# Another order of setup work in a transformer block kernel: fills and later modulations behind the first score operands

## The reference

```python
mod = (silu(c) @ wmod).reshape(8, 6, 1, 256)
sa, ca, ga, sb, cb, gb = (mod[:, i] for i in range(6))
ga, gb = (where(g >= 0, 1, -1) * maximum(abs(g), 0.25) for g in (ga, gb))
h = layernorm(x) * (1 + ca) + sa
x = x + ga * attention(h)        # 16 heads of 16 channels, softmax over 512 keys
h = layernorm(x) * (1 + cb) + sb
x = x + gb * moe(h)              # 2 shared and 16 routed experts, gelu, top 4 of 16
```

## Time and profile before

| | |
|---|---|
| time, median of 3 runs (lowest, highest) | 909.97 us (909.76, 910.23) |
| the profiled execution | 910.85 us |
| its span from first to last instruction | 909.0 us |
| PE busy | 846.5 us, 93% |
| DVE busy | 645.1 us, 71% |
| ACT busy | 665.0 us, 73% |
| POOL busy | 396.6 us, 44% |
| chain that ended last | PE 65%, DVE 18%, ACT 9%, POOL 4% |

### The profile page before, as it was taken

How to read it: one execution, slowest core, us unless ns; L and a number is a source line. 1 busy time by engine, 2 the same in 40 slices (tenths; PEclk the granted TensorE clock), 3 DMA queues, 4 the chain that set the end, 5 groups by cost and what they waited for, 6 DMA issues and landing times.

```text
span 909.0 us, 19413 instructions
## 1 busy us (share of the span) xinstructions
PE 846.5 (93%) x7652; PEld 450.6 (50%) x7652; DVE 645.1 (71%) x1252; ACT 665.0 (73%) x1125; POOL 396.6 (44%) x331
## 2 busy tenths in 40 slices
PE   4878887999999999999999999999999999998998
PEld 4322133365445555565545555566555554555455
DVE  7856577677688878777788777876787778544332
ACT  3488777878788788878788787788886777854342
POOL 5373224234544453444635453444535253347353
PEclk9988889999999999999999999999999999999999
DMA  7043500531217102450217102450233300420140
GB/s 252 2 115 104 140 1 30 175 66 48 76 54 206 52 1 89 129 145 26 83 53 206 48 19 82 147 141 13 70 113 105 111 2 3 151 94 1 64 154 25
DMA packets 47290, 77.18 MB, mean 85 GB/s; under 512 B 6392, under 2 KB 41432, under 8 KB 43104
## 3 DMA queue, kind: packets, MB, share of 16 engines
q1 hardware_dynamic: 47200, 75.94, 27.3%
HBM read 63.47 MB, written 12.34 MB: 83 GB/s over the span
## 4 chain that ended last, share of the span: by engine, by line
PE 65%; DVE 18%; ACT 9%; issue 4%; POOL 4%; ACTq 0%; DVEq 0%; POOLq 0%
PE scalar_bank L945 18%; PE down_bank L1106 17%; DVE neg_max L902 7%; PE vector_bank L1025 6%; PE vector_bank L1008 6%; PE scalar_bank L1008 6%; PE vector_bank L945 5%; DVE rows L758 3%; ACT q_aug L692 3%; DVE gelu L889 2%; PE scalar_bank L1037 2%; POOL act_lo L650 2%; PE vector_bank L1043 2%; ACT gelu L741 2%; DVE o_raw L893 1%
## 5 line engine op out<-in xcount | busy, mean ns | idle before, releaser
L902 DVE TENSOR_REDUCE neg_max<-vector_bank 128x1 f16<-128x512 f32 x484 | 305.8, 684 | 51.3 <-PE vector_bank L1008 44.6
L706 ACT ACTIVATE probs<-scalar_bank 128x512 f32<-128x512 f32 x486 | 260.5, 603 | 48.8 <-PE scalar_bank L1008 44.5
L650 POOL TENSOR_TENSOR act_lo<-gelu,act_hi 128x512 f16<-128x512 f32 x144 | 180.7, 1275 | 136.4 <-ACT act_hi L683 123.1
L1106 PE MATMUL down_bank<-down_hi,act_hi 64*128 64x256 f16 x1120 | 179.1, 270 | 1.9 <-DVE rows L877 1.5
L1106 PE MATMUL down_bank<-down_hi,act_lo 64*128 64x256 f16 x1120 | 178.2, 269 | 0.0
L1106 PE MATMUL down_bank<-down_lo,act_hi 64*128 64x256 f16 x1120 | 178.2, 269 | 0.0
L889 DVE TENSOR_TENSOR gelu<-gelu,gates 128x512 f32<-128x512 f32 x128 | 116.7, 928 | 65.8 <-ACT gelu L741 65.2
L1008 PE MATMUL vector_bank<-k_aug,q_aug 64*128 64x512 f16 x484 | 133.6, 392 | 11.1 <-DVE neg_max L902 6.0
L1008 PE MATMUL scalar_bank<-q_aug,k_aug 64*128 64x512 f16 x486 | 134.2, 387 | 5.2 <-ACT f_ring L669 2.4
L741 ACT ACTIVATE gelu<-scalar_bank 128x512 f32<-128x512 f32 x144 | 84.7, 596 | 70.5 <-PE scalar_bank L945 39.4
L1025 PE MATMUL vector_bank<-probs,v_aug 128*32 128x512 f32 x992 | 118.5, 601 | 0.0
(11 more groups left out here) (193 smaller groups left out, 1259.6 us busy)
## 6 DMA issues: line engine op xcount, KB each, us to landing
gates<-gates_by_expert SPq DMA_DIRECT2D x32, 1024.0 KB, 4.9
q_aug<-q_parts SPq DMA_DIRECT2D x90, 64.0 KB, 3.4
k_aug<-k_parts SPq DMA_DIRECT2D x90, 64.0 KB, 4.1
x_pre<-in_x SPq DMA_DIRECT2D x8, 512.0 KB, 5.9
x_post<-in_x SPq DMA_DIRECT2D x8, 512.0 KB, 5.4
out<-x_post SPq DMA_DIRECT2D x16, 256.0 KB, 2.5
gates<-in_w_up SPq DMA_DIRECT2D x4, 576.0 KB, 10.6
gates<-in_w_down SPq DMA_DIRECT2D x4, 576.0 KB, 3.9
```

The costliest lines, as they stand in the source:

```text
L650: pool.tensor_tensor(act[1][:, c, :], gelu[:, n % NGELU, :], act[0][:, c, :], ALU.subtract).then_inc(s_elo, 1)
L706: scalar.activation(probs[:, n % U, :], src[:], ACT.Exp, scale=SCALE).then_inc(taken[kind], 1)
L902: dve.tensor_reduce(neg_max[:, (u // 2) % TT, at:at + 1], src[:], AX.X, ALU.max, negate=True).then_inc(done, 1)
L1106: ins = pe.matmul(o, act[a][at:at + 64, act_slot(b, c), tok:tok + P], wd[w][at:at + 64, c, :], start=n == 0 and k == 0, stop=c == NEX - 1 ...
```

## The change

Nothing is computed otherwise; instructions change their place or their engine.

- POOL's fills of `q_aug[1]` and `k_aug[1]` move from setup into a new item `fill`, placed at 3.0 of the first group, and POOL also fills `v_aug` there, with two instructions where DVE had eight.
- `late` leaves `HEAD` and is placed at 4.0 of the first group. The q and k bias matmuls leave it for PE's setup, between `modulations(0)` and `h1T`. The second half of the weights' low parts (`w4_lo(1)`) joins `late` on DVE.
- The fourfold identity is made by ACT instead of DVE. DVE finishes silu ahead of the selection columns.
- `bqk` is loaded third instead of sixth, on a semaphore of its own.

```diff
-HEAD = [("x_pre", 0, 1), ("h1T", 0, 0), ("h1T", 1, 0), ("late", 0, 0), ("first", 0, 0), ("first", 1, 0), ("first", 2, 0), ("first", 3, 0)]
+HEAD = [("x_pre", 0, 1), ("h1T", 0, 0), ("h1T", 1, 0), ("first", 0, 0), ("first", 1, 0), ("first", 2, 0), ("first", 3, 0)]
-EARLY = {("first", 4): 3.35, ("first", 5): 5.32, ("first", 6): 9.51, ("first", 7): 11.99, ("qk", 2): 11.62, ("qk_out",
+EARLY = {("late", 0): 4.0, ("fill", 0): 3.0, ("first", 4): 3.35, ("first", 5): 5.32, ("first", 6): 9.51, ("first", 7): 11.99, ("qk", 2): 11.62, ("qk_out",
...
+            sp.dma_start(bqk[:], bqk_in).then_inc(s_bqk, 16)
             mods = wmod.rearrange("(c p) n -> p c n", c=DC)
...
-            pool.memset(q_aug[1][:].bitcast(U32), 0).then_inc(s_aug1, 1)
-            pool.memset(k_aug[1][:].bitcast(U32), 0x3C003C00).then_inc(s_aug1, 1)
...
+                if kind == "fill":
+                    pool.memset(q_aug[1][:].bitcast(U32), 0).then_inc(s_aug1, 1)
+                    pool.memset(k_aug[1][:].bitcast(U32), 0x3C003C00).then_inc(s_aug1, 1)
+                    for m in v_aug:
+                        pool.memset(m[:], 1.0).then_inc(s_aug1, 1)
...
+            scalar.wait_ge(s_const, 6)
+            scalar.activation(four_times(ident_wide), ident[:].rearrange("p (h d) -> p h d", d=DH).unsqueeze(2).broadcast_to([P, 8, 4, DH]),
+                              ACT.Copy).then_inc(s_rep, 1)
...
                 if kind == "late":
+                    w4_lo(1)
                     dve.wait_ge(s_setup_mm, 2)
...
-                    for n in range(2):
-                        for kc in range(TT):
-                            dve.memset(v_aug[n][:, kc, :], 1.0).then_inc(s_aug1, 1)
...
             pe.wait_ge(s_const, 7)
+            pe.wait_ge(s_rep, 1)
+            pe.wait_ge(s_bqk, 16)
+            for pair in range(4):
+                ins = pe.matmul(DB[1][:, 2 * pair:2 * pair + 2], ident_wide[:, P * pair:P * (pair + 1)], bqk[:, 0:4:2], start=True, stop=True)
+            ins.then_inc(s_pickT, 1)
```

More of the change, by code:

```diff
@@ L427, in block_kernel @@
         s_w4, s_mod_in = [sem("wqk_loaded"), sem("wvo_loaded")], [sem("mod0_loaded"), sem("mod1_loaded")]
-        s_small, s_w4hi = sem("biases_loaded"), sem("w4_hi")
+        s_bqk, s_small, s_w4hi = sem("qk_biases_loaded"), sem("biases_loaded"), sem("w4_hi")
         s_w4s, s_silu, s_setup_mm, s_setup_v = sem("w4_split"), sem("silu_steps"), sem("mods_made"), sem("setup_vector")
@@ L497, in _ @@
                              wqkvo[2 * m:2 * m + 2].rearrange("w (c p) n -> p (w c) n", c=DC)).then_inc(s_w4[m], 16)
-            sp.dma_start(bqk[:], bqk_in).then_inc(s_small, 16)
             sp.dma_start(bv_all[:], bv.partition_broadcast(P)).then_inc(s_small, 16)
@@ L523, in _ @@
                         sp.wait_ge(s_aug0, 2)
-                        sp.wait_ge(s_aug1, 2 + 2 * TT)
+                        sp.wait_ge(s_aug1, 4)
                     wait(sp, s_qkst[t], 64, b, 32 * m)
@@ L607, in _ @@
                 z, x_post = z2[b % 2], x_post2[b % 2]
-                if kind == "wsplit":
+                if kind == "fill":
[3 more added lines that the diff above has]
+                        pool.memset(m[:], 1.0).then_inc(s_aug1, 1)
+                elif kind == "wsplit":
                     pool.wait_ge(s_whi, n + 1)
@@ L759, in ln_rows @@
                                       ALU.subtract, ALU.mult).then_inc(s_ln, 1)
+            dve.wait_ge(s_silu, 1)
+            dve.tensor_scalar(silu_t, silu_t, 1.0, None, ALU.add).then_inc(s_silu, 1)
+            dve.wait_ge(s_silu, 2)
+            dve.reciprocal(silu_t, silu_t).then_inc(s_silu, 1)
+            dve.wait_ge(s_silu, 3)
+            dve.tensor_tensor(silu, silu_t, ct_st, ALU.mult).then_inc(s_silu, 1)
             dve.wait_ge(s_const, 6)
-            dve.tensor_copy(four_times(ident_wide), ident[:].rearrange("p (h d) -> p h d", d=DH).unsqueeze(2).broadcast_to([P, 8, 4, DH])
-                            ).then_inc(s_rep, 1)
             dve.tensor_reduce(pick[:, 0:4, 0], ident[:].rearrange("p (x r d) -> p r x d", x=2, r=4), AX.XY, ALU.add).then_inc(s_pick, 1)
@@ L775, in _ @@
             dve.wait_ge(s_pick, 7)
[L776 to L781, removed]
             ln_stats(x_pre, stats, mv[0], s_ln1, 0, s_xpre, 16, 16)
@@ L788, in _, with w4_lo @@
                 dve.tensor_scalar(mods[:, :, n:n + 2], made_mods[:, :, n:n + 2], add, None, ALU.add).then_inc(s_mod0, 1)
-            for m in range(2):
+            def w4_lo(m):
                 lo4, hi4 = (w4[k][:, 2 * m:2 * m + 2].rearrange("p w c n -> p (w c n)") for k in (1, 0))
@@ L794, in _ @@
                                   ALU.subtract).then_inc(s_w4s, 1)
[L795 to L798, removed]
+            w4_lo(0)
+            dve.wait_ge(s_w4s, 1)
+            for k in range(4):
+                dve.tensor_copy(four_times(wide[1][:, k, :]), first_heads(w4[1][:, k // DC, k % DC, :])).then_inc(s_wide[1], 1)
             dve.wait_ge(s_pickT, 1)
@@ L924, in _ @@
                     if n == 0:
-                        dve.wait_ge(s_aug1, 2 + 2 * TT)
+                        dve.wait_ge(s_aug1, 4)
                         wait(dve, made["pv"], G * TT, b - 1, 0)
@@ L982, in _ @@
                 if kind == "late":
[L983 to L987, removed]
+                    pe.wait_ge(s_small, 48)
                     pe.wait_ge(s_mod0, 2)
```

2 lines of the change are left out of this document (1 added, 1 removed).

## The result

| | before | changed |
|---|---|---|
| time, median (lowest, highest) | 910.01 us (909.29, 912.04), 19 runs | 913.12 us (910.01, 915.74), 19 runs |
| the profiled execution | 910.85 us | 912.78 us |
| its span | 909.0 us | 910.9 us |

The ratio is 1.0029, 95% interval 1.0018 to 1.004: the changed kernel is 0.3% slower, where I forecast 909.0, 0.1% faster. Two things stand out before any row is read. The profiled execution lost 1.9 us, the median 3.1; and the changed kernel spreads over 5.7 us, the kernel before over 2.8.

The account below looks back on a forecast made before the run. Over the first 50 us it took a chain of waits through DVE and PE as the bound. Terms -8.2 + 1.5 + 5.7 - 0.5 + 0.5 = -1.0 took the profiled 910.85 to 909.85, median 909.0; range 906.8 to 911.6.

Parts of the forecast that it names:

- The front: Setup up to the first products: they start at 17.6 us instead of 25.88, -8.2 us.
- Slow products: First products after setup: 10 run at the low PE clock, first max tile 7.5 us behind the first product, +1.5 us.
- Late between the maxima: Between eighth and ninth maximum: modulations, gates and DVE's work on them make the ninth maximum 5.7 us later.
- rival (a): Late modulation and gate matmuls between the maxima run at the low clock: +3.1 us, 912.1; chance 15%.
- Clock behind the late work: Behind the late work: PE's clock may fall, `first` 6 taking 2.6 us instead of 1.3; +0.5 us, between 0 and 1.0.
- Fills and refill: Among the maxima: POOL's 5.6 us of fills cost nothing; PE's three ready tiles speed the last 8 maxima, -0.5 us.
- From one execution to the median: Whole kernel: profiled execution stood 0.88 us above the median, so a sum of 909.85 should mean a median of 909.0.

## Why the prediction was wrong

**The front: the step that failed.** "With `bqk`'s transfer ahead of it I take 7.2 (bounds 6.8 and 7.6)." It was 9.05, 8.96 and 8.75 in three profiles, outside both bounds, and 7.10 with `bqk` back. I priced 2 KB at 0.4 us, and chose the upper bound by doubling my own guess, which no row stood behind. What it costs is 0.54 for the issue on SP and 1.5 on `wmod`'s landing (6.7 behind it, 5.2 without it). The first part could be read in the kernel before, where SP takes 0.4 us and more for each issue; the second could not, since the 6.5 us that `bqk` took to land there were spent behind the loads of `wmod` and `wqkvo`. Every other step of the front held: silu, rows at 11.90 (forecast 11.9), bias matmuls 1.85 for 1.50, products 5.29 behind the transposes (5.3). By the trace it is worth 1.8 of the 4.1 us between forecast and median; by time, 1.1 (this kernel) and 2.1 (with `late` ahead), each known only to about 2 us. It isn't the whole error: with `bqk` sixth the median is still 912.0, 3 us above the forecast.

**Slow products: right in kind, 0.6 too large.** Forecast 7.5 behind the first product, measured 6.9 and 7.8 in two executions, 7.1 and 8.0 in the two runs with `bqk` sixth. Seven products were slow in one, eleven in the other, where I had taken ten. The run with seven products ahead of them (5.57) shows the cause: what stands ahead of the products decides their clock.

**Late between the maxima: a second step that failed. The mechanism and its size at the high clock are right, the fall ahead of it was put at nothing.** With the clock held, the ninth maximum came 11.15 behind the first tile, twice; I had 11.5. What I left out is that the clock can fall at `first` 4, before `late`. I had looked for a fall only behind it, and for rival (a) only in the late matmuls, which kept the high level, but for their first few tenths, in every profile with `late` between the maxima but the one with PE kept busy. It added 1.2 to the term. Rival (a) put the same cause in the wrong place, with a price of 3.1.

**Clock behind the late work.** It fell at `first` 6, which I had left undecided between 0 and 1.0 at +0.5; it cost 1.1. It fell at `first` 6 or in the tiles just ahead of it in all five profiles with `late` between the maxima, but for the one with PE kept busy there: at 41 to 43 us in four, and at about 36 in the fifth.

**Fills and refill: right.** POOL's 5.7 us of fills cost nothing beside the maxima.

**From one execution to the median.** The profiled execution of before stood 0.8 above its median, that of after 0.3 below; I moved the forecast by the first and could not know the second. That is 1.2 of the 4.1. That a profile's sum is the median's was an assumption, and the changed kernel's wider spread breaks it. Why it spreads more isn't shown: `late` moved alone has as low a granted clock in its profile (0.980) and spread over 2.5 us in six runs.

**The place of `late` was the decision.** The front gave 6.4 and `late` took 6.9. A sum of two large terms of opposite sign, each right to about 20%, can't tell the sign of a 0.1% result. The same `late` at 14.5 costs 1.65: 906.3, or 904.7 with the front kept busy. What stays open is where the time between 912.8 and 915.7 goes in the slower executions, none of which has a profile. A fall of the clock between 155 and 167 us, which four other profiles have and the two of this kernel don't, is a candidate.

## What to carry to other kernels

Before work is moved off one critical path, ask what waits last at the place where it lands: here a row of maxima on DVE that PE feeds with three banks, where the work cost 4.9 us, while 10 us later it cost 1.65. Ask too whether it has to move: with `late` left where it was, the other parts of the change and `bqk` sixth, the kernel was as fast as the better of the two moves. Don't price a small transfer by its bytes, and keep it behind the load that the first matmul waits for. Where a setup leaves TensorE idle and then gives it its first wide products on the path, a handful of unread wide products in the idle time can pay (3.2 us here; in a second kernel 1.6, within the noise), but in the middle of the work they did not. And look for the clock's falls in the whole trace, not only where the change is: where one stood far behind it, half of a gain was gone.

## What the runs showed of the hardware that was not expected

- 2 KB, 16 bytes for each of 128 partitions, issued one place ahead of a 512 KB load, delayed PE's start by about 1.8 us: it came at 8.71 to 9.05 in four profiles with the small load ahead, at 6.87 to 7.24 in the six of these kernels with it behind. Of this 0.54 is the issue on SP.
- A DVE operation of 16 elements per partition took 3.06 us beside two fills of POOL, and the four normalisations 4.58 for 1.38: both ended only behind the second fill.
- The column of the granted clock reads 1.00 from 12 to 24 us in the changed kernel while the products from 19.45 to 21.54 stand 0.43 apart, as it did before. Durations decide there.
- Two executions of one program part by 1.6 us within one 12 us stretch, since the clock fell at `first` 4 in one of them and not in the other.
- Low stretches far behind the change move too: a fall between 155 and 167 us is in four of twelve profiles, and what lies behind the first group is 0.4 to 2.5 us longer in these.
